# Weights prepared by contraction chunks from a transposed copy, two token blocks projected as the chunks arrive, and the row mean entering by a row of weight sums

## The chip, the cores and the metric

The kernel runs on one core of a Trainium2 chip. The metric is the device time of one execution in microseconds (us); lower is better. All numbers come from timed runs of the kernel before and from one profiled execution of it.

## The reference

What is computed, cut to what matters (x has 2048 rows of 1024, in f32; all matrices are 1024 x 1024):

```python
x = L0_attn_data                                  # (4, 512, 1024)
ln = (x - mean(x)) / sqrt(var(x) + 1e-5)          # over the last axis
block_mask = mask.reshape(32, 32, 32, 32).sum(axis=(1, 3)) > 0   # 32 x 32 squares
w_masked = weight * repeat(repeat(block_mask, 32, 0), 32, 1)
x = x + einsum('bsk,nk->bsn', ln, w_masked)       # the projection
z = (x - mean(x)) / sqrt(var(x) + 1e-5)
logits = z @ W_gate + b_gate                      # 8 experts
top_idx = top_k(logits, 2)
y = relu(einsum('bsd,edh->bseh', z, W_e) + b_e)   # of the two chosen experts
x = x + y.mean over the two
```

## The kernel before, in words

The 2048 rows are 16 token blocks of 128 (`NB`). The kernel has two stages. In the first, each token block is projected, normalised and routed; in the second, 38 blocks of 128 gathered rows go through their experts. Both stages are matrix multiplication in f32r split into a rounded part (HI) and its remainder (LO), in three passes (`PASSES`: HI by HI, HI by LO, LO by HI). A pass over one half (512 columns) of a token block is 8 matmuls, one for each chunk of 128 of the contraction; a block is 2 halves of 3 passes, 48 matmuls.

Every engine has one instruction list, executed in order; semaphores are counted (`wait_ge`, `then_inc`). So an instruction that waits holds up all that stands behind it on its engine.

Before the first projection the weight is prepared, in eight stripes `r` of 128 output rows, each through a chain over all engines. SyncE (SP) loads the mask stripe and the weight stripe, 512 KB each. VectorE (DVE) sums the mask over groups of 32 columns (`sum_mask`, L862); TensorE (PE) sums over groups of 32 rows with a 0/1 matrix (`group_sums`, L353); DVE compares with 0 (`element_mask`, L873); GpSimd (POOL) multiplies the weight stripe with the mask (L1053); ScalarE (ACT) takes the row mean (`mean`, L561) and subtracts it (`centre`, L566), because with centred weight rows the mean of a token drops out of the product; PE transposes the stripe in eight pieces into PSUM (`transpose_w`, L362); ACT copies it, rounded, to `wT` HI (`w_hi`, L571); DVE writes the remainder to `wT` LO (`w_lo`, L868), with one input in PSUM and one in SBUF. PE also multiplies each masked stripe with the gate weights (`fold_w`, L396) so that the logits can be had from x itself. The first half of block 0 is projected after four stripes (`PASS_AT`), the second after all eight. `warm` (L386) is a run of dummy matmuls at the start.

The transposed token blocks come from the host as `data_t`. For each block t, ACT copies them, rounded, to `xT` HI (`x_hi`, L555) and DVE writes the remainder (`x_lo`, L719). ACT computes mean and squares of the row block (`stats1`, L601 and L603), POOL the inverse deviation `kept` (`inverse_std1`, L1020 and L1022). After the projection of a half, DVE adds it, scaled, to the rows (`residual`, L727), and takes the statistics of the sum (`stats2`, L708 and L714), POOL computes `inverse_std2`, ACT writes the normalised rows (L632). The gate product (L475) and the logits (L460) run on PE between the halves; DVE selects two experts (`top2`) and turns positions into one-hot tables (`one_hots`, L775 to L788), PE puts them into the queue (`enqueue`, L380; `positions`, L449).

Each block of the loop is on PE: logits of block i-1, half 0 of block i, `enqueue(i-2)`, the gate product of block i, `positions(i-1)`, half 1 of block i. Half n of block i waits only for `residual(i-1, n)`, which frees the accumulator. ACT has in each turn: `x_hi(i+1)`, the normalised rows, in turns 10 to 14 one or two pieces of the first expert's weight (L637, their remainders on POOL are L1069), `gated` (L641), `stats1(i+1)`.

Of the kernel before, what the change touches and what calls it, by code (L numbers as in the profile page):

```python
# [5 lines left out]
F32 = mybir.dt.float32  # L6
# [15 lines left out]
def build(nc, data, weight, mask, w_gate, b_gate, w_e, b_e, data_t, out):  # L22
# [14 lines left out]
    SNAP = 7  # L37
    N_LATE = N_BLOCKS - EARLY
# [7 lines left out]
    with ctx:  # L46
# [24 lines left out]
        mask_stage = at("mask_stage", [P, NT, D], I32, slot_base + NT * D * 4)  # L71
        w0_stage = at("w0_stage", [P, KT, H], F32, slot_base + slot_bytes // 2)
# [12 lines left out]
        group = sb("group", [P, P], F32)  # L85
        msum_offset = cursor[0]
        msum = sb("msum", [P, NT, NSUB], F32)
        emask = sb("emask", [P, NT, NSUB], F32)
# [14 lines left out]
        fold = sb("fold", [P, 2 * N_EXP], F32)  # L103
# [4 lines left out]
        foldedT = at("foldedT", [P, QUARTER], F32, rows_b_offset)  # L108
        kept = sb("kept", [P, NB], F32)
        minus_mean = sb("minus_mean", [P, NT], F32)  # L110
# [10 lines left out]
        rs = sb("rs", [P, 2, 4], F32)  # L121
# [37 lines left out]
        assert cursor[0] <= msum_offset + 2 * NT * NSUB * 4  # L159
# [61 lines left out]
        l_x, l_raw, l_bias = (even_odd(n) for n in ("l_x", "l_raw", "l_bias"))  # L221
        l_xr, l_x1 = ([sem(f"{n}_{i}") for i in range(3)] for n in ("l_xr", "l_x1"))
# [3 lines left out]
        c_msum, c_em, c_wm, c_wlo = sem("c_msum"), sem("c_em"), sem("c_wm"), sem("c_wlo")  # L226
        c_masked, c_mean = sem("c_masked"), sem("c_mean")
        c_group, c_wt, c_whi = sem("c_group"), sem("c_wt"), sem("c_whi")
# [13 lines left out]
        ST, TOP, HOT, RS1, RS2, GATES = 3, 11, 7, 2, 4, 4  # L242
# [8 lines left out]
        def w_half_of(r):  # L251
            return r % 2

        def x_side(t):
            return psT[:, 0, :, :] if t == NB else xb[:, t % 2, :].rearrange("p (k t) -> p k t", t=P)
# [4 lines left out]
        PASS_AT = NT // 2  # L260
        X0_AT = 4
        WARM = (16, 24, 24)
# [3 lines left out]
        def _(eng):  # L266
            def load_x(t):
                if t >= 2:
                    eng.wait_ge(c_xlo, t - 1)
                    eng.wait_ge(c_gate, t - 1)  # L270
                eng.dma_start(xb[:, t % 2, :], data_t[t]).then_inc(l_x[t % 2], 16)

            for r in range(NT):
                rows = slice(r * P, (r + 1) * P)
                if r == X0_AT:
                    load_x(0)
                eng.dma_start(mask_stage[:, r, :], mask[rows, :]).then_inc(s_m[r], 16)  # L277
                eng.dma_start(w_stage[:, r, :], weight[rows, :]).then_inc(s_w[r], 16)  # L278
# [4 lines left out]
            eng.wait_ge(s_spare, 16)  # L283
# [11 lines left out]
            for i in range(-1, NB + 1):  # L295
                t = i + 1
                if t < NB:
                    if t >= 3:
                        eng.wait_ge(l_x1[t % 3], 16 * (t // 3))
                        eng.wait_ge(c_ln2, t - 2)  # L300
# [829 lines left out]
```

## Time and profile before

| | us |
|---|---|
| median of 3 timed runs | 703.81 |
| lowest and highest | 702.95 and 704.12 |
| the profiled execution's own time | 703.16 |
| its span, from first to last instruction | 701.4 |
| PE busy in the span | 678.8 (97%) |
| DVE, ACT, POOL busy | 297.3, 276.5, 289.2 |
| mean granted TensorE clock | 0.994 |

Time lies outside the span by 1.8 us. A busy time of PE is the time in which some matmul was under way; it tells where PE had no work at all, and not that its work was useful.

### The profile page before, as it was taken

Reading aid. Unit: us, or ns where it says so; the run is one execution under the profiler, and the core shown is the slowest. Engines: PE = TensorE matmul, PEld = TensorE weight load, DVE = VectorE, ACT = ScalarE, POOL = GpSimd, SP = SyncE. Lnnn points to the kernel's source line nnn. Section 1 sums busy time; section 2 is a strip of 40 time slices with the busy share of each in tenths; the row PEclk is TensorE's granted clock in tenths of the full one; section 3 lists DMA queues with packets and bytes.
Section 4 is the critical chain, followed back from the end, with each engine's and each line's share of the span. In section 5 each row is a group of like instructions: output and inputs, shape, how many; then the busy total and the mean of one; then the engine's idle time right before and its main releaser. Section 6 shows DMA issues by size and latency. Waiting matters only on the chain.

```text
span 701.4 us, 11208 instructions
## 1 busy us (share of the span) xinstructions
PE 678.8 (97%) x3617; PEld 558.5 (80%) x3617; DVE 297.3 (42%) x572; ACT 276.5 (39%) x387; POOL 289.2 (41%) x256
## 2 busy tenths in 40 slices
PE   6799999999999999999999999999999999999993
PEld 5568888788888888888888888888888888888882
DVE  4657675777986563342450640360542430000000
ACT  4964343435553334333333333343434343434330
POOL 5512111124763245635363645353545453434330
PEclk9999999999999999999999999999999999999997
DMA  8825445388844388687684774685784854232323
GB/s 314 317 89 189 175 152 209 128 292 270 267 156 151 121 217 252 141 252 163 177 238 125 199 224 82 173 242 135 187 259 97 230 133 110 42 53 38 54 36 54
DMA packets 34501, 118.21 MB, mean 169 GB/s; under 512 B 5776, under 2 KB 5776, under 8 KB 34448
## 3 DMA queue, kind: packets, MB, share of 16 engines
q1 hardware_dynamic: 22032, 80.23, 32.2%
q0 software_dynamic: 11232, 37.23, 26.2%
q8 instruction: 34, 0.56, 0.3%
q10 hardware_dynamic: 1184, 0.04, 0.1%
q14 instruction: 19, 0.16, 0.1%
HBM read 83.40 MB, written 37.75 MB: 173 GB/s over the span
## 4 chain that ended last, share of the span: by engine, by line
PE 94%; DMA 2%; SPq 1%; ACT 0%; DVE 0%; POOLq 0%; issue 0%
PE psO L339 86%; PE psT L442 5%; DMA mask_stage<-L_attn_mask 2%; PE psG L475 1%; SPq L278 1%; SPq L277 1%; PE psT L380 0%; PE psT L460 0%; ACT wT L571 0%; PE psT L362 0%; POOLq L46 0%; PE psS L449 0%; DVE wT L868 0%; DVE msum L862 0%; ACT xb L679 0%
## 5 line engine op out<-in xcount | busy, mean ns | idle before, releaser
L339 PE MATMUL psO<-slots,xT 128*128 (+1 forms) x1872 | 436.2, 392 | 0.0
L339 PEld LDWEIGHTS psO<-slots,xT 128*128 128x128 f32 x1872 | 348.3, 188 | 70.8
L339 PE MATMUL psO<-wT,xT 128*128 128x512 f32 x768 | 182.7, 394 | 0.2 <-ACT wT L571 0.2
L339 PEld LDWEIGHTS psO<-wT,xT 128*128 128x128 f32 x768 | 141.7, 188 | 28.5 <-ACT wT L571 0.3
L1083 POOL DMA_INDIRECT rows_out<-xb,tok_of x37 | 63.1, 1706 | 222.6 <-ACT xb L679 215.2
L679 ACT ACTIVATE xb<-psO 128x512 f32<-128x512 f32 x78 | 46.6, 598 | 253.2 <-PE psO L339 253.2
L850 DVE CAST slots<-raw 128x1024 fp32r<-128x1024 f32 x56 | 56.2, 1003 | 193.5 <-PE psO L339 105.0
L1077 POOL TENSOR_TENSOR xT<-x2T,xT 128x1024 fp32r<-128x1024 f32 x38 | 99.5, 2619 | 18.3 <-ACT x2T L658 18.0
L852 DVE TENSOR_TENSOR slots<-raw,slots 128x1024 fp32r<-128x1024 f32 x56 | 73.1, 1305 | 1.9
L617 ACT ACTIVATE psO<-bias_slot 128x512 f32 (+1 forms) x78 | 47.0, 602 | 37.3 <-ACT xb L679 15.2
L653 ACT ACTIVATE xT<-psT 128x1024 fp32r<-128x1024 f32 x38 | 38.4, 1011 | 7.1 <-PE psT L442 7.1
L658 ACT ACTIVATE x2T<-psT 128x1024 f32<-128x1024 f32 x38 | 38.7, 1017 | 0.0
L1020 POOL TENSOR_SCALAR rs<-squares 128x1 f32<-128x1 f32 x16 | 8.6, 538 | 68.1 <-ACT psT L603 67.9
L555 ACT ACTIVATE xT<-xb 128x1024 fp32r<-128x1024 f32 x16 | 17.0, 1060 | 42.4 <-PE psO L339 40.5
L1032 POOL TENSOR_SCALAR rs<-mv 128x1 f32<-128x1 f32 x16 | 3.8, 236 | 57.9 <-DVE mv L714 46.5
L1045 POOL DMA_INDIRECT x<-x_rows,tok_of x19 | 23.7, 1248 | 6.2 <-DVE tok_of L950 3.1
L1069 POOL TENSOR_TENSOR slots<-w_stage,slots 128x1024 fp32r<-128x1024 f32 x8 | 19.2, 2410 | 9.5 <-ACT slots L637 9.5
L727 DVE SCALAR_TENSOR_TENSOR xr<-psO,kept,xr 128x512 f32<-128x512 f32 x22 | 16.4, 746 | 14.8 <-PE psO L339 14.5
L632 ACT ACTIVATE x<-xr,rs 128x1024 f32<-128x1024 f32 x11 | 13.7, 1242 | 21.9 <-POOL rs L1037 21.9
L719 DVE TENSOR_TENSOR xT<-xb,xT 128x1024 fp32r<-128x1024 f32 x16 | 19.5, 1218 | 1.9 <-ACT xT L555 1.9
L1053 POOL TENSOR_TENSOR w_stage<-w_stage,emask 128x1024 f32<-128x1024 f32 x8 | 15.3, 1912 | 12.1 <-DVE emask L873 12.1
L442 PEld LDWEIGHTS psT<-ident,x 128*128 128x128 f32 x152 | 17.7, 140 | 2.5
(167 smaller groups left out, 448.7 us busy)
## 6 DMA issues: line engine op xcount, KB each, us to landing
raw<-L_ffn_W_e SPq DMA_DIRECT2D x56, 512.0 KB
xb<-data_t SPq DMA_DIRECT2D x16, 512.0 KB, 4.2
x_rows<-x SPq DMA_DIRECT2D x16, 512.0 KB, 5.0
xr<-L_attn_data SPq DMA_DIRECT2D x11, 512.0 KB, 5.7
rows_out<-xr SPq DMA_DIRECT2D x11, 512.0 KB, 2.7
mask_stage<-L_attn_mask SPq DMA_DIRECT2D x8, 512.0 KB, 11.1
w_stage<-L_attn_weight SPq DMA_DIRECT2D x8, 512.0 KB, 11.7
bias_slot<-L_ffn_b_e SPq DMA_DIRECT2D x8, 512.0 KB
```

Source lines behind the costliest of these rows:

```text
L339: last = eng.matmul(psum, xT[:, p, a, kt, :], moving(b, kt), start=(i == 0 and kt == 0 and not seeded), stop=(i == len(PASSES) - 1 and kt ...
L442: last = eng.transpose(psT[:, turn_bank(b), kt, :], rows_of(b, slice(kt * P, (kt + 1) * P)), ident[:])
L617: eng.activation(psO[:, n, :], bias, ACT.Copy).then_inc(c_seed, 1)
L653: eng.activation(xT[:, b % 2, HI, :, :], psT[:, turn_bank(b), :, :], ACT.Copy).then_inc(c_rhi, 1)
L658: eng.activation(x2T[:], psT[:, turn_bank(b), :, :], ACT.Copy).then_inc(c_rhi, 1)
L679: eng.activation(xb[:, b % 2, n * HALF:(n + 1) * HALF], psO[:, n, :], ACT.Relu, scale=1.0 / TOP_K).then_inc(c_out, 1)
L719: eng.tensor_tensor(xT[:, t % 2, LO, :, :], x_side(t), xT[:, t % 2, HI, :, :].bitcast(F32), ALU.subtract).then_inc(c_xlo, 1)
L850: eng.tensor_copy(slots[:, e % 2, HI, kt, :], raw[:, kt % 2, :]).then_inc(c_split, 1)
L852: eng.tensor_tensor(slots[:, e % 2, LO, kt, :], raw[:, kt % 2, :], slots[:, e % 2, HI, kt, :].bitcast(F32), ALU.subtract).then_inc(c_split, 1)
L1045: eng.indirect_dma_start(rows_of(b), None, x2_rows[0:known, :], bass.IndirectOffsetOnAxis(ap=tok_col(b), axis=0), bounds_check=known - 1, ...
L1077: eng.tensor_tensor(xT[:, b % 2, LO, :, :], x2T[:], xT[:, b % 2, HI, :, :].bitcast(F32), ALU.subtract).then_inc(c_rlo, 1)
L1083: eng.indirect_dma_start(out, bass.IndirectOffsetOnAxis(ap=tok_col(b), axis=0), xb[:, b % 2, :], None, bounds_check=N_TOK + P - 1, compute ...
```

## The change

The host passes two more arrays: `weight_t`, the transposed weight, and `mask_blocks`, the mask reordered so that the 1024 elements of one 32 by 32 square lie in one row, and a tile of 128 rows holds the squares of one contraction chunk (128 values of k, all output columns). The weight is prepared by chunk `c` of the contraction, directly in the layout that the product reads:

- A chunk's squares are summed, 1024 to 1, on DVE (`sum_blocks`) or, for chunks 1, 3 and 5, on ACT (`block_sums`); DVE turns the sum into a row of 32 flags with a comparison against a diagonal table (`blocks_of`, a tensor_tensor with both inputs in SBUF); PE spreads it over the 128 partitions (`spread_k`, f16); ACT copies it out (`mask_k`); POOL multiplies the chunk of `weight_t`; ACT rounds it (`w_hi`); DVE takes the remainder (`w_lo`), now with both inputs in SBUF. `mean`, `centre` and the 64 transposes are gone.
- Blocks 0 and 1 are projected together, chunk by chunk (`chunk_hh`, `chunk_lh`, `chunk_hl`), 12 matmuls a chunk, into four PSUM halves (`acc`).
- The weight rows are loaded a second time, untransposed, behind the chunks (`load_w`), masked (`mask_rows`, six on DVE, two on POOL) with row sums, for `fold_w` and for the sums. `row_of_sums` on PE makes a row of weight sums, the same in all partitions.
- The mean of a token block comes in by that row: for blocks 0 to 3 ACT scales it (`move_mean`) and POOL adds it to the finished rows (`correct`); for blocks 4 to 15 ACT writes it, scaled, into the accumulator ahead of the first pass (`seed_mean`), and the passes add to it. Each half then waits for `seed_mean`, which waits for `residual`.
- The order of all engines for blocks 2 to 6 is written out by hand; gates, logits and expert selection of blocks 0 to 3 are done later and together (`top2_first`, `places_first`, `hots_first`). From turn 7 (`LOOP`) the loop is as before, with `seed_mean` added. The expert stage is unchanged.

The core of the diff:

```diff
-        WARM = (16, 24, 24)
+        WARM = (24, 40)
+        SUMS_ACT = (1, 3, 5)
+        ROWS_POOL = (2, 5)
 # SP
+            load_mask(0)
+            load_wt(0)
+            load_x(0)
+            load_mask(1)
+            load_mask(2)
+            load_wt(1)
             load_x(1)
+            for c in range(3, KT):
+                load_mask(c)
+                load_wt(c - 1)
+            load_wt(KT - 1)
+            load_rows(0)
+            load_x(2)
+            load_rows(1)
+            load_w(0)
...
 # PE
+            def chunk(i, c, t):
+                part_x, part_w = PASSES[i]
+                for n in range(NH):
+                    mm = eng.matmul(acc(t, n), xT[:, t, part_x, c, :], wT[:, part_w, c, n * HALF:(n + 1) * HALF],
+                                    start=(i == 0 and c == 0), stop=(i == 1 and c == KT - 1))
...
+            warm(WARM[0])
+            spread_k(0)
+            warm(WARM[1])
+            spread_k(1)
+            chunk_hh(0, 0)
+            chunk_lh(0, 0)
+            chunk_hl(0, 0)
...
+            for c in range(2, KT - 1):
+                if c < 4:
+                    spread_k(c + 2)
+                chunk_hh(c, 0)
+                chunk_hh(c, 1)
+                if c >= 4 and c + 2 < KT:
+                    spread_k(c + 2)
+                if c == KT - 2:
+                    spread_n()
+                chunk_lh(c, 0)
+                chunk_lh(c, 1)
+                chunk_hl(c, 0)
+                chunk_hl(c, 1)
...
+                if i == 0 and t >= FIRST:
+                    eng.wait_ge(c_sown, NH * (t - FIRST) + n + 1)
...
+            project_pass(2, 0, 0)
+            project_pass(2, 0, 1)
+            fold_w(0)
+            fold_w(1)
+            project_pass(2, 0, 2)
+            fold_w(2)
+            project_pass(2, 1, 0)
+            fold_w(3)
+            row_of_sums(0)
+            row_of_sums(1)
...
 # ACT
+            def seed_mean(t, n):
...
+                eng.wait_ge(c_res, NH * (t - 1) + n + 1)
+                eng.activation(psO[:, n, :], sum_row[:, n * HALF:(n + 1) * HALF], ACT.Copy,
+                               scale=minus_mean1[:, t:t + 1]).then_inc(c_sown, 1)
...
+            mask_k(6)
+            w_hi(5)
+            mask_k(7)
+            w_hi(6)
+            mean1(0)
+            w_hi(7)
 # DVE
+            def blocks_of(c):
...
+                eng.tensor_tensor(blocks_k[:, c, :], block_sum[:, c:c + 1].to_broadcast([P, NSUB]), off_diagonal[:],
+                                  ALU.is_gt).then_inc(c_blocks, 1)
+            def w_lo(c):
+                eng.wait_ge(c_whi, c + 1)
+                eng.tensor_tensor(wT[:, LO, c, :], w_stage[:, c, :], wT[:, HI, c, :].bitcast(F32), ALU.subtract).then_inc(c_wlo, 1)
...
+            blocks_of(3)
+            sum_blocks(4)
+            w_lo(2)
+            blocks_of(5)
             w_lo(3)
+            sum_blocks(6)
+            sum_blocks(7)
...
 # POOL
+            for c in range(KT):
+                eng.wait_ge(c_kmask, c + 1)
+                eng.wait_ge(s_w[c], 16)
+                rows = w_stage[:, c, :].rearrange("p (g s) -> p g s", s=SUB)
+                eng.tensor_tensor(rows, rows, k_mask[:, c, :].unsqueeze(2).to_broadcast([P, NSUB, SUB]), ALU.mult).then_inc(c_masked, 1)
+            inverse_std1(0)
+            mask_rows(2)
```

## Rows read from the trace of the kernel before

**Rows 1.** Busy time by stretch: us, then PE, PEld, DVE, ACT, POOL, clock, DMA

```profile
0.00:47.06 47.06, 35.30 (x279) 27.02 (x280) 25.32 (x42) 31.70 (x42) 20.44 (x38) 1.00 0.62 235
47.06:229.33 182.27, 182.27 (x1137) 147.61 (x1137) 134.81 (x382) 79.97 (x114) 58.24 (x100) 1.00 0.58 200
```

**Rows 2.** Chain that ended last: start us, us, what

```profile
9.81 17.06 DMA mask_stage<-L_attn_mask
...
28.58 5.58 PE psO L339 x24
...
41.80 0.22 PE psG L425 x2
...
47.06 5.56 PE psO L339 x24
52.62 0.57 PE psG L475 x16
53.20 0.11 PE psS L449
...
64.61 0.20 PE psT L380 x8
...
95.40 0.13 PE psT L460 x2
...
107.57 0.13 PE psT L460 x2
```

**Rows 3.** Timeline of PE, first 48 us: start, us, engine, line, operation

```profile
7.91 2.75 PE L386 MATMUL psT<-tri,ones 128*128 128x128 f16 x24
...
34.96 0.62 PE L396 MATMUL psS<-w_stage,wg 128*8 128x256 f32 x8
35.51 1.09 PE L362 MATMUL psT<-ident,w_stage 128*128 128x128 f32 x8
```

**Rows 4.** Timeline of DVE, first 62 us

```profile
11.41 1.22 DVE L862 TENSOR_REDUCE msum<-mask_stage 128x32 f32<-128x1024 int32 x1 [0.15 <-DMA mask_stage<-L_attn_mask]
...
26.90 1.22 DVE L862 TENSOR_REDUCE msum<-mask_stage 128x32 f32<-128x1024 int32 x1 [0.65 <-DMA mask_stage<-L_attn_mask]
...
30.40 1.21 DVE L868 TENSOR_TENSOR wT<-psT,wT 128x1024 fp32r<-128x1024 f32 x1
...
56.07 1.22 DVE L785 TENSOR_TENSOR row_hot<-lane,pos_r 128x1024 f16<-128x1024 f16 x1
```

**Rows 5.** Timeline of POOL, first 62 us

```profile
30.56 1.92 POOL L1053 TENSOR_TENSOR w_stage<-w_stage,emask 128x1024 f32<-128x1024 f32 x1 [2.31 <-DVE emask L873]
...
49.38 0.55 POOL L1022 TENSOR_TENSOR kept<-rs,half_neg 128x1 f32<-128x1 f32 x1
...
56.29 1.42 POOL L1022 TENSOR_TENSOR kept<-rs,half_neg 128x1 f32<-128x1 f32 x1
```

**Rows 6.** Timeline of DVE, 168 to 188 us

```profile
175.88 0.16 DVE L777 TENSOR_TENSOR count<-count,psS 128x8 f32<-128x8 f32 x1
175.96 0.72 DVE L778 TENSOR_TENSOR pos_r<-pos_i,low_bits 128x8 int32<-128x8 int32 x1
...
176.79 2.38 DVE L783 TENSOR_TENSOR blk_hot<-lane,pos_j 128x128 f16<-128x128 f16 x1
```

**Rows 7.** Timeline of POOL, 172 to 181 us

```profile
174.24 4.78 POOL L1069 TENSOR_TENSOR slots<-w_stage,slots 128x1024 fp32r<-128x1024 f32 x2 [2.37 <-ACT slots L637]
```

**Rows 8.** Instructions of line L783: count, durations min/median/max in ns, first and last start

```profile
L783 DVE TENSOR_TENSOR blk_hot<-lane,pos_j x16: 291/292/2384, 55.9 to 236.7; 128x128 f16<-128x128 f16 x16
```

**Rows 9.** Timeline of ACT, first 62 us

```profile
28.07 1.05 ACT L561 ACTIVATE rows_a<-w_stage 128x1024 f32<-128x1024 f32 x1
...
38.60 1.02 ACT L571 ACTIVATE wT<-psT 128x1024 fp32r<-128x1024 f32 x1 [0.56 <-PE psT L362]
```

**Rows 10.** Timeline of ACT, 168 to 196 us

```profile
177.39 0.19 ACT L603 ACTIVATION_READ_ACCUMULATOR psT<-xr,minus_mean 128x1 f32 x1
...
180.67 1.06 ACT L555 ACTIVATE xT<-xb 128x1024 fp32r<-128x1024 f32 x1 [3.09 <-PE psO L339]
```

More of the change, by code:

```diff
@@ L19, with build @@
 PASSES = [(HI, HI), (HI, LO), (LO, HI)]
-def build(nc, data, weight, mask, w_gate, b_gate, w_e, b_e, data_t, out):
+def build(nc, data, weight, w_gate, b_gate, w_e, b_e, data_t, weight_t, mask_blocks, out):
     N_TOK, D = data.shape
@@ L37, in build @@
     SNAP = 7
+    FIRST = 4
+    LOOP = 7
     N_LATE = N_BLOCKS - EARLY
@@ L431, in transpose_rows @@
+            positions(4)
+            enqueue(2)
+            project_pass(6, 0, 0)
+            logits(5)
+            project_pass(6, 0, 1)
+            enqueue(3)
+            project_pass(6, 0, 2)
+            gate(6)
+            project_pass(6, 1, 0)
+            enqueue(4)
+            project_pass(6, 1, 1)
+            project_pass(6, 1, 2)
+            positions(5)
             def transpose_rows(b):
@@ new lines, in _ @@
+            block_sums(5)
+            w_hi(3)
+            mask_k(5)
+            w_hi(4)
+            mask_k(6)
[4 more added lines that the diff above has]
+            w_hi(7)
+            square1(0)
+            eng.wait_ge(c_spread_n, 1)
+            eng.activation(n_mask[:].rearrange("p r g -> p (r g)"), psD, ACT.Copy).then_inc(c_nmask, 1)
+            x_hi(2)
+            x_hi(3)
+            stats1(1)
+            for r in range(5):
+                sum_diagonal(r)
@@ L606, in seed_half @@
+            gate_out(4)
+            mean1(5)
+            norm2(3)
+            seed_mean(5, 0)
+            square1(5)
+            x_hi(6)
+            seed_mean(5, 1)
+            norm2(4)
+            gate_out(5)
+            stats1(6)
+            seed_mean(6, 0)
+            x_hi(7)
+            seed_mean(6, 1)
+            norm2(5)
+            stats1(7)
+            gate_out(6)
+            seed_mean(7, 0)
             def seed_half(b, slot, n):
@@ L878, in _ @@
[L878 to L892 removed]
+            FAR = 3.0e38
@@ new lines, in _ @@
+            sum_blocks(6)
+            sum_blocks(7)
+            eng.wait_ge(c_prep, 4)
+            eng.tensor_tensor(blocks_n[:], block_sum[:].unsqueeze(2).to_broadcast([P, KT, P // SUB]),
+                              off_group[:].unsqueeze(1).to_broadcast([P, KT, P // SUB]), ALU.is_gt).then_inc(c_blocks, 1)
+            for c in range(4, KT):
+                w_lo(c)
+            mask_rows(0)
+            mask_rows(1)
+            x_lo(2)
+            residual(0, 0)
+            residual(0, 1)
@@ new lines, in _ @@
+            stats2(3)
+            top2_first()
+            residual(4, 0)
+            stats2_half(4, 0)
+            places_first()
+            hots_first(0)
+            residual(4, 1)
+            stats2_half(4, 1)
+            stats2(4)
+            x_lo(6)
+            hots_first(1)
+            hots_first(2)
+            top2(4)
+            residual(5, 0)
+            stats2_half(5, 0)
+            hots_first(3)
+            residual(5, 1)
+            stats2_half(5, 1)
+            stats2(5)
@@ L907, in _ @@
+            x_lo(7)
+            one_hots(4)
+            top2(5)
+            residual(6, 0)
+            stats2_half(6, 0)
+            one_hots(5)
+            for i in range(LOOP, NB + 1):
+                residual(i - 1, 1)
+                stats2_half(i - 1, 1)
+                stats2(i - 1)
+                top2(i - 1)
                 if i + 1 <= NB:
```

855 lines of the change are left out of this document (590 added, 265 removed).

## The prediction

> **What bounds the kernel now.** I read the busy time by stretch first. From 47.06 us on PE is busy in all of the 182.27 us up to the end of the first stage; before 47.06 it is busy 35.30 us, much of it with dummies, transposes and folding [rows 1]. So time can only be won where PE has no projection to do, and that is the start: by 47.06 us one block is projected, 48 matmuls. The chain shows why: it hangs on the mask's arrival for 17.06 us, and afterwards runs on PE without a break [rows 2]. A pass triple of 24 matmuls takes 5.58 us, 0.2325 each; one block 11.16; a turn of the loop with all its small work takes 107.57 - 95.40 = 12.17. The logits ahead of block 6 end at 107.57 + 0.13 = 107.70, where its first matmul starts [rows 2]. The last mask stripe, the 16th transfer, is used at 26.90 and the third, the 5th transfer, at 11.41 [rows 4]: 1.4 us a transfer.
>
> **The change, part by part.**
>
> *Removed.* 64 transposes, the two ACT instructions a stripe for the mean (1.05 for the mean [rows 9] and about as much for the centring). Their PE time lay in time in which PE waited anyway; what counts is when the projection starts.
>
> *Loading.* The last chunk of `weight_t` is the 18th transfer, two behind the last mask tile, which keeps its place: 26.9 + 2 x 1.3 = 29.5 us. Behind it a mask multiplication (1.92 [rows 5]) and a rounding (1.02 [rows 9]) must come: the last chunk could be multiplied from 32.6, and 12 matmuls of 0.2325 (2.79 us) end at 35.4. That is the floor by the loads. 2.79 a chunk on PE stands against 2 x 1.3 of loading, so PE has no reserve to catch up.
>
> *The start.* Constants, 24 dummies (2.75 us [rows 3], to 7.9), the diagonal table (it waits for an ACT instruction of 1.0), the first sum (1.22, to 9.0), flags, spreading at 9.2; then 40 dummies, 40/24 x 2.75 = 4.6 us, to 13.9; chunk 0 runs from 14.1. Going down the lists with these durations chunk 2 could start at 21.4; six chunks of 2.79 and some 0.7 for the spreads give 38.8 as the end of blocks 0 and 1. Call this end T1.
>
> *A lock between DVE and POOL.* The rows show one. A table of 128x128 takes DVE 0.29 and once 2.38 [rows 8]: that one began at 176.79, and POOL had two multiplications of weight under way from 174.24 to 179.02 [rows 6, 7]. The small instruction ahead, at 175.96, took 0.72 and ended as POOL's first one did. Both have two inputs in SBUF. The instruction at 175.88, with one input in PSUM, took its usual 0.16 [rows 6]. The other way round POOL's power took 1.42 where it takes 0.55, beside a DVE instruction with two SBUF inputs that ended at 57.29 [rows 4, 5]. And `w_lo` with its input in PSUM took 1.21 across a mask multiplication at 30.56, which kept its 1.92 [rows 4, 5]. So the old `w_lo` was free of this and the new one isn't, nor are `x_lo` and `blocks_of`.
>
> The Trainium skill says the same on its page "SBUF — State Buffer", section "Who interferes with whom": a VectorE instruction with two SBUF inputs and a GpSimd instruction that reads SBUF exclude each other for the whole instruction. By that rule the new `w_lo` and `blocks_of` are held up for a whole mask multiplication each time; a sum without it would keep T1 at 38.8.
>
> Per chunk the pair must then do 1.92 + 1.21 + 0.15 = 3.3 us, more than PE's 2.79. Worse, the flags of chunk c+1 stand on DVE behind what waits for POOL's chunk c, and PE's spreading, ACT's copy and the next multiplication hang on them. My walk: multiplications of chunks 2 to 7 at 19.9, 22.5, 25.8, 29.1, 32.5 to 33.9, 37.0 to 38.2; chunk 2 on PE from 24.8. From there PE needs 16.7 + 0.7, to 42.2, and loses some 2 us in chunks 4 and 5: `w_lo(4)` stands on DVE behind the sums of both last mask tiles and behind POOL, and the spreading for chunk 7 stands behind chunk 5's first pass. T1 is 43.8 to 45.6 by who gets the lock in ties. I take 44.
>
> *From T1 on PE.* Up to the first matmul of block 6 it has: blocks 2 to 5, 4 x 11.16 = 44.6; eight foldings of 0.55 (start to start [rows 3]) = 4.4; eight rows of sums, f32 of 128 columns, at half a folding (256 columns) 0.28 = 2.2; the small transposes (0.22 [rows 2]) and two small sums 0.5; six gate products of 0.57 = 3.4 and five logits of 0.13 = 0.7 [rows 2]; three enqueues of 0.20, two positions of 0.11 and a few more for the four blocks [rows 2] = 0.9. Sum 56.7. Before, that matmul stands at 107.70, with one enqueue (0.2) more done. Gain = 107.5 - 56.7 - T1 - S = 50.8 - T1 - S, where S is what PE waits between T1 and block 6. What no row shows: the row of sums could take from 0.13 (logits) to 0.55 (folding) each, 1.2 us less to 2.2 more in all. `mask_rows` with its sum is taken as 1.35 (`w_lo` 1.21 to two halves, 1.5); `correct` on POOL lies between 1.92 [rows 5] and 2.39, half of the 4.78 [rows 7].
>
> *Waits in the hand-written order (S).* Eight `mask_rows`, `correct`, `x_lo` and the expert selection share that lock. `logits(3)` on PE stands behind `gated` of block 3 on ACT, which stands behind `norm2(1)` and `seed_mean(4, 1)`, and these behind POOL's corrections: 0 to 1.2 us. `seed_mean(5, 0)` needs `residual(4, 0)`, behind the selection of four blocks at once on DVE (some 3 us, from POOL's last deviation): 0.3 to 1.2. `positions(4)` and `seed_mean(6, 0)` stand behind `hots_first(2)`, which needs `enqueue(1)`, and `top2(4)`: 1.3 to 2.1. S is 1.6 to 4.5; I take 3. The row weights land by about 46 us at 1.3 each, ahead of their use: cover enough.
>
> *The loop from turn 7.* Same matmuls. `seed_mean` (half of 1.0 plus, about 0.6) comes behind `stats1` on ACT. In a turn with weight pieces ACT ends its statistics at 177.58 and starts `x_hi` at 180.67 [rows 10]; the next half needs the seed just ahead of that: 2.5 us of cover remain. Cost nothing; without the cover, its lateness in every turn. The expert stage moves as a whole.
>
> *Sum.* 50.8 - 44 - 3 = 3.8 us, against the profiled execution's own 703.16 (span 701.4 and 1.8 around it). The median of the runs is 0.65 above it; taken off the median: 700.0 us.
>
> **The rivals.**
>
> *The lock costs little* (0.22): instructions interleave luckily, T1 38.8 and S 2 give a gain of 10: 693.8. For it: POOL's multiplications reach the lock only when flags come, and PE hides some. Against it: the flags themselves are under the lock.
>
> *The loads are the floor* (0.06): T1 35.4, S near 0.5, gain 15: 689. Against it the 40 dummies, and PE's 2.79 a chunk.
>
> *The gain is used up* (0.13): T1 45.6 and S 4.5 give 0.7: 703.1, no change.
>
> *The hand-written order starves PE* (0.08): one wrong place costs more than I found. `mask_rows` 4 to 7 stand among residuals on DVE; if these come 5 us later than PE's foldings want them, S is 8: T1 44 gives a loss of 1.2, 705. It decides from S = 6.8 on.
>
> *`seed_mean` becomes PE's bound in every turn* (0.06), the other side: if ACT's chain slips by more than 2.5 us, each of nine turns waits. At 1 us a turn more than covered that is 9 us, minus the 3.8: 709. It decides from 0.42 us a turn. Against it: ACT is idle 3.1 us just there [rows 10].
>
> The forecast itself has 0.45, its own range 698 to 702.
>
> **How the numbers follow.** A change of under 0.2%, 1.4 us, can't be told from none here. Faster: 0.45 + 0.22 + 0.06 and a little of the used-up case, 0.75. Same: 0.11. Slower: 0.08 + 0.06, 0.14. The range 691 to 704.5 holds the forecast, the used-up case and most of the one without a lock; it leaves out the floor, `seed_mean` as the bound and the outer part of starvation, together under 0.2.
>
> **What would show it.** In the profile after: the end of the 96th chunk matmul (T1) at 44, 38.8 or 35; `w_lo` longer than 1.21 where POOL multiplies, up to 3.1; `blocks_of` up to 2; mask multiplications 3.3 apart in the middle. Block 6's first matmul at 103.9 instead of 107.70. Turns of 12.17 from there on, PE without gaps. Wrong would be: a granted clock that falls in the waits of the start (it is 1.00 in the first 47 us now, with PE idle for 11.8 of them [rows 1]), turns longer than 12.17, or a T1 on time and a gain lost behind it.

## The result, and the profile after

| us | before | after |
|---|---|---|
| median of the runs (9 each) | 703.33 | 705.32 |
| lowest and highest | 702.94, 704.12 | 704.89, 705.80 |
| profiled execution, its span | 703.16, 701.4 | 705.06, 703.3 |

The changed kernel is slower: ratio 1.0027, interval 1.0017 to 1.0038. The forecast was 700.0, faster.

The busy time by stretch of the kernel after (us, then PE, PEld, DVE, ACT, POOL, clock, DMA), beside [rows 1]:

```profile
0.00:47.06 47.06, 36.88 (x188) 28.36 (x189) 34.60 (x43) 22.88 (x36) 26.65 (x38) 0.93 0.91 345
14.00:18.00 4.00, 1.55 (x5) 0.97 (x4) 4.00 (x4) 2.11 (x2) 1.60 (x1) 0.80 1.03 410
18.00:22.00 4.00, 4.00 (x12) 2.80 (x11) 2.79 (x3) 1.23 (x3) 1.92 (x1) 0.50 1.03 410
22.00:26.00 4.00, 3.82 (x16) 2.66 (x15) 1.48 (x3) 2.09 (x4) 1.81 (x1) 0.85 1.03 410
47.06:107.70 60.64, 56.96 (x409) 41.23 (x408) 39.90 (x83) 36.63 (x60) 26.35 (x42) 1.00 0.47 176
107.70:229.33 121.63, 120.64 (x765) 97.10 (x765) 96.52 (x270) 64.66 (x94) 48.14 (x68) 1.00 0.58 203
```

Two things are new. The granted clock is 0.50, 1.2 GHz, between 18 and 22 us, where it was 1.00 before. And behind 47.06 PE is no longer without a gap: 3.7 us are idle up to 107.70, 1.0 behind it.

The timeline of PE of the kernel after shows where:

```profile
16.84 1.22 PE L490 MATMUL psO<-wT,xT 128*128 128x512 f32 x2 [2.45 <-DVE wT L1299]
...
29.06 0.19 PE L476 MATMUL psS<-blocks_k,group 128*128 128x32 f16 x1 [0.63 <-DVE blocks_k L1294]
...
44.40 3.91 PE L457 MATMUL psT<-wT,xT 128*128 128x512 f32 x16
...
91.24 0.19 PE L668 MATMUL psS<-chosen,tri 128*128 128x32 f16 x1 [0.70 <-DVE chosen L1197]
...
93.03 3.89 PE L457 MATMUL psO<-wT,xT 128*128 128x512 f32 x16 [1.43 <-ACT psO L883]
...
107.52 2.09 PE L457 MATMUL psO<-wT,xT 128*128 128x512 f32 x8 [1.35 <-ACT psO L883]
...
226.40 5.74 PE L457 MATMUL psO<-wT,xT 128*128 128x512 f32 x24 [0.80 <-ACT psO L883]
...
231.98 0.29 PE L575 MATMUL psT<-diagonal,gated 128*128 128x16 f32 x2
```

T1, the end of blocks 0 and 1, is 44.40, where the first pass of L457 starts. Block 6's first matmul is the row at 107.52. Before, the chain puts it at 107.70 [rows 2] and PE's timeline at 107.55, so nothing was gained up to there, and the rest loses: the last logits start at 231.98, and at 229.93 before, 2.05 later. The span grew by 1.9.

The lock of the prediction is there. The timeline of DVE of the kernel after (L1294 is `blocks_of`, L1299 `w_lo`, L1557 the mask multiplication):

```profile
13.92 1.73 DVE L1294 TENSOR_TENSOR blocks_k<-block_sum,off_diagonal 128x32 f16<-128x32 f32 x1
15.57 1.21 DVE L1299 TENSOR_TENSOR wT<-w_stage,wT 128x1024 fp32r<-128x1024 f32 x1
...
27.11 1.90 DVE L1294 TENSOR_TENSOR blocks_k<-block_sum,off_diagonal 128x32 f16<-128x32 f32 x1
...
33.34 4.08 DVE L1299 TENSOR_TENSOR wT<-w_stage,wT 128x1024 fp32r<-128x1024 f32 x2
```

And POOL's multiplication of chunk 1:

```profile
13.69 1.92 POOL L1557 TENSOR_TENSOR w_stage<-w_stage,k_mask 128x1024 f32<-128x1024 f32 x1 [2.11 <-ACT k_mask L821]
```

A flag row of 0.18 took 1.73: it began while POOL's multiplication of 13.69 to 15.61 was under way and ended with it. Behind it on DVE stood `w_lo(0)`, for which PE then waited 2.45 us. In that wait the clock fell.

### The profile page after: what moved, and what is told of

Read it like the earlier page. It is cut to its first block, busy times and chain, and to the rows that moved or that the text cites. A ratio compares the mean times of both kernels' runs of the same rounds, so it can differ in the third digit from the quotient of the medians.

```text
span 703.3 us, 11125 instructions
## 1 busy us (share of the span) xinstructions
PE 677.6 (96%) x3571; PEld 552.2 (79%) x3571; DVE 310.5 (44%) x543; ACT 289.1 (41%) x420; POOL 309.5 (44%) x266
## 4 chain that ended last, share of the span: by engine, by line
PE 89%; DVE 5%; issue 2%; ACT 1%; POOL 1%; POOLq 0%; ACTq 0%; DVEq 0%
PE psO L457 78%; PE psT L718 5%; PE psT L457 2%; PE psO L490 1%; PE psT L490 1%; DVE wT L1299 1%; PE psG L563 1%; DVE xT L1089 1%; DVE blocks_k L1294 1%; DVE block_sum L1285 1%; PE psS L545 1%; DVE st L1078 0%; ACT psO L883 0%; PE psT L531 0%; PE psT L554 0%
## 5 line engine op out<-in xcount | busy, mean ns | idle before, releaser
L457 PE MATMUL psO<-slots,xT 128*128 (+1 forms) x1872 | 436.1, 392 | 0.0
L457 PEld LDWEIGHTS psO<-slots,xT 128*128 128x128 f32 x1872 | 348.3, 188 | 70.7
L457 PE MATMUL psO<-wT,xT 128*128 128x512 f32 x624 | 151.5, 396 | 3.6 <-ACT psO L883 3.6
L457 PEld LDWEIGHTS psO<-wT,xT 128*128 128x128 f32 x624 | 114.4, 188 | 27.6 <-issue 4.3
L1598 POOL TENSOR_TENSOR xT<-x2T,xT 128x1024 fp32r<-128x1024 f32 x38 | 98.0, 2580 | 18.3 <-ACT x2T L1025 18.2
L1277 DVE TENSOR_TENSOR slots<-raw,slots 128x1024 fp32r<-128x1024 f32 x56 | 74.9, 1337 | 1.9
L1525 POOL TENSOR_SCALAR rs<-mv 128x1 f32<-128x1 f32 x16 | 5.3, 334 | 54.6 <-DVE mv L1084 54.5
L1557 POOL TENSOR_TENSOR w_stage<-w_stage,k_mask 128x1024 f32<-128x1024 f32 x8 | 18.0, 2249 | 16.1 <-ACT k_mask L821 16.1
L1590 POOL TENSOR_TENSOR slots<-w_stage,slots 128x1024 fp32r<-128x1024 f32 x8 | 19.2, 2413 | 9.5 <-ACT slots L1006 9.5
L811 ACT ACTIVATE xT<-xb 128x1024 fp32r<-128x1024 f32 x12 | 12.7, 1056 | 21.0 <-PE psO L457 17.7
L883 ACT ACTIVATE psO<-raw,minus_mean 128x512 f32<-128x512 f32 x24 | 16.3, 679 | 9.6 <-DVE xr L1097 6.0
L490 PE MATMUL psO<-wT,xT 128*128 128x512 f32 x48 | 16.8, 448 | 3.2 <-DVE wT L1299 3.0
L718 PE MATMUL psT<-ident,x 128*128 128x128 f32 x152 | 19.7, 272 | 0.0
```

The lines of the kernel that those rows point to most:

```text
L457: last = eng.matmul(psum, xT[:, p, a, kt, :], moving(b, kt), start=(i == 0 and kt == 0 and not seeded), stop=(i == len(PASSES) - 1 and kt ...
L490: mm = eng.matmul(acc(t, n), xT[:, t, part_x, c, :], wT[:, part_w, c, n * HALF:(n + 1) * HALF], start=(i == 0 and c == 0), stop=(i == 1 an ...
L718: last = eng.transpose(psT[:, turn_bank(b), kt, :], rows_of(b, slice(kt * P, (kt + 1) * P)), ident[:])
L1277: eng.tensor_tensor(slots[:, e % 2, LO, kt, :], raw[:, kt % 2, :], slots[:, e % 2, HI, kt, :].bitcast(F32), ALU.subtract).then_inc(c_split, 1)
L1598: eng.tensor_tensor(xT[:, b % 2, LO, :, :], x2T[:], xT[:, b % 2, HI, :, :].bitcast(F32), ALU.subtract).then_inc(c_rlo, 1)
```

## The experiments

Every kernel was timed against the kernel before on its own chip, whose median was 703.25 to 703.40. The first five start from the kernel after, each with one edit. "The wait for `w_lo(0)`" is PE's 2.45 us at 14.4 to 16.8.

**Dummies in the wait for `w_lo(0)`**

```diff
             chunk_lh(0, 0)
+            warm(20)
             chunk_hl(0, 0)
```

> Edit: 20 more dummy matmuls (about 2.3 us) on PE between chunk_lh(0, 0) and chunk_hl(0, 0), where PE of the changed kernel stands still for 2.45 us up to 16.84 and its granted clock then reads 0.50 from 18 to 22 us. Theory A (the wait lets the clock fall, and the slow matmuls of chunks 0 and 1, 0.43 us each where 0.23 is usual, delay the spreading for chunk 3): the clock stays 1.00, spread_k(3) comes 2 us earlier than its 23.68, and the end of blocks 0 and 1 (T1, now 44.40) comes 1.5 to 2.5 us earlier; the time falls by 1 to 2.5 us. Rival B (the lock between DVE and POOL alone sets the pace of the chunks, the clock is hidden): the clock is 1.00, T1 moves by under 0.5 us and the time is unchanged. Rival C (what is won at T1 is given back in the hand-written order of blocks 2 to 6): T1 earlier by 2, time within 0.5 us.

Measured: 703.68, ratio 1.000 (0.9991 to 1.001), span 702.0. The clock stayed at 1.00 up to T1, and T1 is 41.38, 3.0 earlier. Only 1.3 of the 3.0 reached the end. The windows of this kernel at 90 us show why:

```profile
90.00:92.00 2.00, 1.99 (x6) 1.64 (x7) 1.97 (x6) 1.98 (x3) 0.73 (x2) 0.64 0.00 0
92.00:94.00 2.00, 2.00 (x6) 1.54 (x6) 1.86 (x4) 0.69 (x1) 0.61 (x2) 0.50 0.31 127
```

And PE's timeline there:

```profile
88.22 0.19 PE L669 MATMUL psS<-chosen,tri 128*128 128x32 f16 x1 [0.71 <-DVE chosen L1198]
...
90.01 5.50 PE L457 MATMUL psO<-wT,xT 128*128 128x512 f32 x16 [1.43 <-ACT psO L884]
```

The same two waits as in the kernel after (0.71, 1.43) were now followed by the lower clock: the 16 matmuls took 5.50, and 3.89 there. So the clock's fall is worth 3.0 us at T1, and the later waits can cost 1.6 more than they last. In the medians of the timed runs the edit is worth 1.6 (705.32 and 703.68).

**Flags with one tensor input in SBUF**, as a tensor_scalar

```diff
-                eng.tensor_tensor(blocks_k[:, c, :], block_sum[:, c:c + 1].to_broadcast([P, NSUB]), off_diagonal[:],
-                                  ALU.is_gt).then_inc(c_blocks, 1)
+                eng.tensor_scalar(blocks_k[:, c, :], off_diagonal[:], block_sum[:, c:c + 1], None, ALU.is_lt).then_inc(c_blocks, 1)
```

> Edit: the flags of a chunk by one tensor_scalar (table below the chunk's sum, the sum as a per-partition scalar), so with one tensor input in SBUF in place of two. Theory A (the lock needs two SBUF inputs on DVE, and the flags behind POOL's multiplications hold up the chain spreading, copy, next multiplication): every instance takes under 0.3 us where four now take 0.66 to 1.90, spread_k(4) and (5) no longer wait (0.63 us at 29.06 now), T1 falls from 44.4 to 41.5 to 43; the time falls by 1 to 2 us if the rest follows. Rival B (DVE waits for POOL whatever its inputs): some instances stay near 2 us and T1 stays. Rival C (T1 earlier, but the order of blocks 2 to 6 gives it back): T1 earlier, time within 0.5 us.

Measured: 705.19, ratio 1.0022 (1.0013 to 1.0031). DVE's rows of this kernel:

```profile
14.00 1.93 DVE L1294 TENSOR_SCALAR blocks_k<-off_diagonal,block_sum 128x32 f16<-128x32 f32 x1
20.26 0.96 DVE L1294 TENSOR_SCALAR blocks_k<-off_diagonal,block_sum 128x32 f16<-128x32 f32 x1 [0.93 <-ACT rows_a L817]
22.38 0.24 DVE L1294 TENSOR_SCALAR blocks_k<-off_diagonal,block_sum 128x32 f16<-128x32 f32 x1
```

The flags were held as before, 1.93, with a table and a scalar for each partition, both in SBUF. This form doesn't escape the lock: the wait for `w_lo(0)` stayed (2.16), and so did the one for a flag row (0.62, at 27.98). T1 is 43.37; the clock fell here too, for a shorter stretch (0.64 from 18 to 22 us, 1.00 from 22 to 26). The Trainium skill, "SBUF — State Buffer", section "Who interferes with whom", names tensor_scalar among the operations that can use VectorE's second port and then contend; the 1.93 agrees, though the trace doesn't show in which way the instruction read its inputs.

**Residuals ahead of the expert selection**

```diff
 # POOL
-            inverse_std2(3)
             inverse_std1(4)
+            inverse_std2(3)
 # DVE
-            top2_first()
             residual(4, 0)
+            top2_first()
             stats2_half(4, 0)
...
-            hots_first(2)
-            top2(4)
             residual(5, 0)
+            hots_first(2)
+            top2(4)
```

> Edit: order alone. DVE adds half 0 of block 4 before the selection of four blocks and half 0 of block 5 before hots_first(2), instead of behind; POOL computes the deviation of block 4 before block 3's second one. Theory A (PE's 1.43 us before block 5 and 1.35 before block 6 are seed_mean standing behind a residual that stands behind selection work): both gaps vanish (the first leaves the 0.7 us for the selection's matmuls), and as PE never waits again before turn 7 the time falls by 2.3 to 2.8 us, to just below the kernel before. Rival B (other waits take their place: positions, enqueue, later blocks): the gaps vanish but reappear within the next two blocks, and the time falls by under 1 us.

Measured: 701.00, ratio 0.9964 (0.9952 to 0.9975), span 699.6. The waits of 1.43 and 1.35 are gone, 0.69 for `chosen` stays. The PE timeline of this kernel has the first pass of block 5 directly behind the small matmuls:

```profile
90.58 0.19 PE L668 MATMUL psS<-chosen,tri 128*128 128x32 f16 x1 [0.69 <-DVE chosen L1197]
...
90.79 3.90 PE L457 MATMUL psO<-wT,xT 128*128 128x512 f32 x16
```

The span is 3.7 shorter: T1 is 43.74, 0.7 earlier, which this edit doesn't explain (the start ran a little differently), and from T1 to block 6 it is 60.0 instead of 63.1, 2.8 of it the two waits. So the order of a few instructions of DVE and POOL, each under a microsecond, was worth 3.0 us.

**The seed of the last half ahead of `x_hi(16)`**

```diff
                 if i + 1 <= NB:
                     x_hi(i + 1)
-                if i < NB:
+                if i < NB - 1:
                     seed_mean(i, 1)
```

with `if i == NB - 1: seed_mean(i, 1)` ahead of these lines.

> Edit: order alone. In the last turn ACT writes the seed of block 15's half 1 before x_hi(16), which waits for the transposed rows of the expert stage. Theory A (PE's 0.80 us at 226.40 is this seed standing behind x_hi(16)): the gap vanishes and the time falls by 0.8 to 1.0 us. Rival B (x_hi(16) coming 0.7 us later delays the first expert's passes by as much): the gap vanishes and comes back before the expert stage, time unchanged.

Measured: 704.12, ratio 1.001 (1.0001 to 1.0019), span 701.1. The last turn takes 13.01 (logits at 216.71 and 229.72), as before, where the kernel after has 14.00. In this profile the clock behaved the other way round from the kernel after. The same wait at the start was not followed by the lower clock, T1 is 41.60, but the waits at 90 were:

```profile
16.68 0.73 PE L490 MATMUL psO<-wT,xT 128*128 128x512 f32 x2 [2.45 <-DVE wT L1301]
...
90.20 5.50 PE L457 MATMUL psO<-wT,xT 128*128 128x512 f32 x16 [1.42 <-ACT psO L883]
```

Of the program's order nothing differs up to 90 us. So the fall of the clock is not fixed by the program: these waits expose the kernel to it, execution by execution. The 11 timed runs say the same: four took 702.8 to 703.0 at a mean clock of 0.993, seven took 704.0 to 704.6 at 0.990 to 0.991. With the dummies none of 11 was below 0.992; the nine of the kernel after were all at 0.988 to 0.990. This also confirms T1: without the fall it is 41.4 to 41.6, with and without dummies.

**Jobs exchanged**: DVE multiplies by the mask, read straight from the PSUM tile that PE spread it into, and POOL takes the remainder `w_lo`; `mask_k` on ACT goes, `spread_k` now waits for DVE's multiplications, and `spread_n` comes one place later.

```diff
 # DVE
+            def mask_chunk(c):
+                eng.wait_ge(c_spread, c + 1)
+                eng.wait_ge(s_w[c], 16)
+                rows = w_stage[:, c, :].rearrange("p (g s) -> p g s", s=SUB)
+                eng.tensor_tensor(rows, rows, psB(c).unsqueeze(2).to_broadcast([P, NSUB, SUB]), ALU.mult).then_inc(c_masked, 1)
 # POOL
             for c in range(KT):
+                eng.wait_ge(c_whi, c + 1)
+                eng.tensor_tensor(wT[:, LO, c, :], w_stage[:, c, :], wT[:, HI, c, :].bitcast(F32), ALU.subtract).then_inc(c_wlo, 1)
```

> Edit: the two engines under the lock change jobs. DVE multiplies the chunk of weight with the spread mask read straight from PSUM (one SBUF input, ACT's copies of the mask go), POOL takes the remainder (two SBUF inputs, 2.4 us where it converts). So beside POOL's remainders DVE has, but for x_lo(0), x_lo(1) and the small flags, no instruction with two SBUF inputs. Theory A (the lock sets the pace of the chunks): chunk 2 starts at 20 to 22 instead of 25.1, POOL's remainders follow each other without being stretched, T1 is 36 to 38.5. Rival B (the loads and the hops between five engines set the pace): T1 stays above 41. What follows T1 is unchanged: if the hand-written order passes all of it on, the time falls by 6 us or more; if its own waits on DVE, ACT and POOL decide (rival C), by 2 to 3.

Measured: 704.55, ratio 1.0012 (1.0003 to 1.002), span 701.5, T1 42.64. POOL's eight remainders are no longer stretched, they take 2.37 to 2.40 each, but PE has seven waits of 0.28 to 1.25 in the chunks (4.0 us in all), and T1 is 1.3 later than with the dummies. The lock is not gone. DVE's flags still have both inputs in SBUF, and four of the rows took 1.21 to 1.87 beside POOL's remainders; one from each timeline:

```profile
12.98 1.87 DVE L1286 TENSOR_TENSOR blocks_k<-block_sum,off_diagonal 128x32 f16<-128x32 f32 x1
```

```profile
12.43 2.37 POOL L1555 TENSOR_TENSOR wT<-w_stage,wT 128x1024 fp32r<-128x1024 f32 x1 [7.31 <-ACT wT L825]
```

So this run doesn't tell the lock's price from that of the chain PE, DVE, ACT, POOL and back.

**Dummies, residuals and last seed together**, the three edits as above.

> Edit: the 20 dummies, the early residuals and the last turn's seed together, nothing else. By the single runs: T1 41.4; the waits before blocks 5 and 6 (1.43 and 1.35) and in the last turn (0.80) gone; and if what slowed the matmuls after those waits in two of the profiles (granted clock 0.50 from 92 to 94 us, 1.6 us lost) was the clock falling in them, no stretch below 1.00 after 30 us. The terms add: span 703.3 - 3.0 - 2.8 - 0.3 - 0.95 = 696.3, time 698. If they overlap (a rival: each uncovers the next wait), 700 or more.

Measured: 698.33 (697.86 to 698.66), ratio 0.9926 (0.9913 to 0.9938), span 696.4. The parts add up: 3.0 for the clock, 3.0 for the residuals, 0.96 for the last seed are 7.0, and 703.3 - 7.0 = 696.3. The clock is 1.00 throughout. PE's timeline of this kernel tells what sets T1:

```profile
16.44 0.73 PE L490 MATMUL psO<-wT,xT 128*128 128x512 f32 x2 [1.25 <-DVE wT L1302]
...
23.05 0.19 PE L476 MATMUL psG<-blocks_k,group 128*128 128x32 f16 x1 [1.31 <-DVE blocks_k L1297]
...
31.57 0.73 PE L490 MATMUL psO<-wT,xT 128*128 128x512 f32 x2 [0.53 <-DVE wT L1302]
...
41.38 0.93 PE L457 MATMUL psT<-wT,xT 128*128 128x512 f32 x3
```

From chunk 2 (23.15) to T1 lie 18.2 us: 72 matmuls at 0.2325 are 16.7, one wait 0.5, and the spreads and changes of operand between them 1.0. So from chunk 2 on PE sets the pace, and the lock costs at most 0.5 there. What else it costs lies ahead of chunk 2: the wait for `w_lo(0)`, of which the dummies leave 1.25, and the 1.31 for a flag row that took 1.35. How much of these waits is the lock's, no run isolates.

**The exchange with these orders**

> Edit: the exchange of jobs between DVE and POOL with the early residuals and the last turn's seed, no dummies added. If T1 of the exchange (36 to 38.5) is passed on: span 692 to 694. If blocks 2 to 6 then wait for row weights, folds and corrections on the other engines, new waits stand on PE between T1 and block 4, and the span is 695 or more.

The edits are those of the two kernels ahead, without dummies. Measured: 699.24, ratio 0.9939 (0.9926 to 0.9952), span 697.4, T1 42.66: 0.9 slower than the one with the jobs as they were. The T1 of 36 to 38.5 on which the expectation rests didn't come. The clock was at 1.00 here (0.60 from 14 to 18 us in the profile of the exchange alone), and T1 is the same: in these two profiles it doesn't hang on the clock.

**Foldings in one run**: the eight `fold_w` and eight `row_of_sums` of the kernel after stand two at a time between passes; here they all follow `project_pass(3, 0, 0)`.

```diff
+            for n in range(2):
+                for i in range(3):
+                    project_pass(2, n, i)
+            project_pass(3, 0, 0)
+            for r in range(NT):
+                fold_w(r)
+            for r in range(NT):
+                row_of_sums(r)
```

> Edit: order of PE alone. The eight foldings and eight rows of sums, spread between the passes of blocks 2 and 3 in the changed kernel, come in one run behind the first pass of block 3. Question: in the changed kernel a pass of 8 matmuls between such small f32 groups takes 2.0 to 2.05 us from start to start of its neighbours, where 8 x 0.2325 is 1.86. Theory A (each change between the two kinds costs some 0.15 us): the passes of block 2 take 1.86, and from T1 to the first logits PE needs 0.8 to 1.0 us less. Rival B (the small groups themselves have been misjudged, the passes are not longer): no difference. The time falls by at most 1 us.

Measured: 702.31 (700.22 to 705.22), ratio 0.9985 (0.9972 to 0.9998), span 698.6, with T1 41.36. PE of this kernel:

```profile
41.36 11.16 PE L457 MATMUL psT<-wT,xT 128*128 128x512 f32 x48
52.36 1.97 PE L457 MATMUL psO<-wT,xT 128*128 128x512 f32 x8
54.27 3.64 PE L545 MATMUL psS<-row_stage,wg 128*8 128x256 f32 x64
57.84 2.05 PE L554 MATMUL psT<-bias_slot,ones 128*128 128x128 f32 x16
59.65 2.08 PE L457 MATMUL psO<-wT,xT 128*128 128x512 f32 x8
```

Eight foldings take 57.84 - 54.27 = 3.57, 0.45 each, and 48 matmuls of the projection 11.00. From T1 to the first logits (73.28 in the kernel after) it is 27.18 against 28.88, so the same matmuls cost 1.7 us less when they aren't mixed, more than theory A had. The span is 4.7 shorter: 3.0 at T1, where the clock stayed at 1.00 in this profile, and these 1.7. The spread of the timed runs, 5 us, fits a clock that falls in none, one or both of the places where PE waits: mean clock 0.995 in the runs of 700.2 to 700.8, 0.990 to 0.993 around 702.3, 0.987 from 704.0 on.

**The flags' table in PSUM**, on top of the three orders: `blocks_of` has one input in SBUF and one in PSUM.

```diff
+        psX = psT[:, 1, KT // 2, 0:NSUB]
-                eng.tensor_tensor(blocks_k[:, c, :], block_sum[:, c:c + 1].to_broadcast([P, NSUB]), off_diagonal[:],
+                eng.tensor_tensor(blocks_k[:, c, :], block_sum[:, c:c + 1].to_broadcast([P, NSUB]), psX,
```

> Edit: the kernel with dummies, early residuals and the last turn's seed (698.33), and the diagonal table that the flags are compared with moved from SBUF to PSUM, so that blocks_of has one input in SBUF and one in PSUM. The tensor_scalar form with its one tensor input in SBUF was still held up to 1.93 us, so the form with fewer SBUF inputs is not the whole rule. Theory A (any DVE instruction with a PSUM input goes free beside POOL, and the held-up flags pace the chunks): every blocks_of takes under 0.25 us, T1 falls from 41.38 to 39.5 to 40.5, the time to 696.5 to 697.5. Rival B (w_lo and x_lo take the lock anyway, POOL's multiplications are then held instead): flags under 0.25 us, T1 within 0.4 of 41.38, time within 0.5 of 698.33.

Measured: 700.29, ratio 0.9951 (0.9938 to 0.9964), span 699.2: worse than with the three orders alone (698.33). The flags are free, 0.17 to 0.19 each, and chunk 2 starts at 22.32. But what was held is now the next DVE instruction with both inputs in SBUF. L1303 is `w_lo` here, L1335 `blocks_n`, the flags for the row weights, whose table stayed in SBUF. DVE first:

```profile
14.02 2.92 DVE L1303 TENSOR_TENSOR wT<-w_stage,wT 128x1024 fp32r<-128x1024 f32 x1
...
24.44 2.81 DVE L1303 TENSOR_TENSOR wT<-w_stage,wT 128x1024 fp32r<-128x1024 f32 x1
...
29.87 1.84 DVE L1335 TENSOR_TENSOR blocks_n<-block_sum,off_group 128x32 f16<-128x32 f32 x1
31.64 2.35 DVE L1303 TENSOR_TENSOR wT<-w_stage,wT 128x1024 fp32r<-128x1024 f32 x2
```

PE, where it waits for `w_lo(4)`, the first of the two at 31.64:

```profile
32.91 0.73 PE L491 MATMUL psO<-wT,xT 128*128 128x512 f32 x2 [2.44 <-DVE wT L1303]
```

POOL's multiplications, with three in a row:

```profile
21.40 7.63 POOL L1561 TENSOR_TENSOR w_stage<-w_stage,k_mask 128x1024 f32<-128x1024 f32 x3 [0.41 <-ACT k_mask L823]
29.76 1.91 POOL L1561 TENSOR_TENSOR w_stage<-w_stage,k_mask 128x1024 f32<-128x1024 f32 x1 [0.73 <-ACT k_mask L823]
```

And the window behind PE's wait:

```profile
34.00:38.00 4.00, 4.00 (x13) 2.86 (x12) 0.95 (x1) 2.12 (x4) 1.85 (x1) 0.57 1.03 410
```

`w_lo(0)` takes 2.92 behind a free flag, where it took 1.21 behind a held one, and PE's pass on it starts at 16.99, no earlier than with the three orders (16.44). `w_lo(3)` takes 2.81, but it isn't what PE waits for at 32.91. That is `w_lo(4)`, and ahead of it stands `blocks_n`, 1.84 beside POOL's multiplication of 29.76 where it took 0.19 with the three orders. PE's pass starts 1.34 later than there (32.91 and 31.57), and in the four microseconds from 34 on the granted clock was 0.57: from that pass to T1 it is 11.36 instead of 9.81. Together that makes T1 44.27 instead of 41.38. Theory B had the flags free and nothing won, but not this loss.

**Exchange, orders and foldings**, with eight dummies, and two sums moved:

```diff
             blocks_of(5)
-            sum_blocks(6)
             mask_chunk(4)
-            sum_blocks(7)
+            sum_blocks(6)
             mask_chunk(5)
+            sum_blocks(7)
```

> Edit: the exchange of jobs again (DVE masks from PSUM, POOL takes remainders), now with the masks of chunks 4 and 5 on DVE ahead of the sums of mask tiles 6 and 7 instead of behind them (in the first try chunk 4 waited at 30.37 for a mask queued behind the tile 6 sum), 8 dummies in chunk 0, early residuals, last turn's seed and the folds in one run. Theory A (with the lock out of the way the loads pace): T1 38 to 39.5 and the time 3 us below the kernel with the same orders and the old jobs. Rival B (the hops PE to DVE to ACT to PE to POOL and PE's own order of spreads pace it): T1 40.5 or more, time no better than that kernel's.

Measured: 697.18, ratio 0.9907 (0.9893 to 0.9922), span 695.5, T1 42.34. That is rival B's T1. The time is 1.2 below the kernel with the three orders, but this one has the foldings in one run as well; against the same with the old jobs, which comes next, it gains nothing.

**Orders and foldings, jobs as in the kernel after**: the edits of dummies, residuals, last seed and foldings.

> Edit: the kernel with dummies, early residuals and the last turn's seed (698.33), and the folds and rows of sums in one run. By the single run from T1 to the first logits it saves 28.90 - 27.18 = 1.7 us. If that carries through: 696.6. If the earlier logits then wait for ACT or the selection on DVE (rival): a part of it, 697.5 or more.

Measured: 696.85 (696.46 to 696.91), ratio 0.9904 (0.9889 to 0.9918), span 694.7, T1 41.46. This is the fastest one. Its first window, with the clock at 1.00:

```profile
0.00:47.06 47.06, 37.51 (x221) 29.64 (x222) 37.11 (x47) 25.87 (x43) 28.45 (x40) 1.00 0.95 372
```

The runs of the two kernels last told don't overlap, but their intervals do; that the unexchanged one is better by 0.3 us rests on 4 runs each.

**The same with the table in PSUM and later positions**

```diff
+            project_pass(5, 0, 0)
             eng.wait_ge(c_top4, 12)
...
-            project_pass(5, 0, 0)
             project_pass(5, 0, 1)
-            enqueue(0)
             project_pass(5, 0, 2)
+            enqueue(0)
```

> Edit: the one before it, plus the flag table in PSUM, plus the position matmuls of the first four blocks behind the first pass of block 5 instead of ahead of it (0.7 us of waiting for the selection), with enqueue(0) one pass later. If all terms add: 696.6 less 1 for the flags less 0.6, 695.0. If the selection chain (hots, enqueues, top2 of block 4) now comes late for positions(4), a wait before block 6 returns and the last term is lost: 695.7.

Measured: 699.07, ratio 0.9932 (0.992 to 0.9944), span 697.4. The table in PSUM brings back the wait of 2.44 (at 32.49), with `blocks_n` taking 1.85, the lower clock behind it (0.69 from 34 to 38 us) and T1 43.83. `w_lo(3)` took 2.09 here and the wait is the same, so it doesn't come from the 2.81. The later positions end the wait of 0.70 ahead of them and leave one of 0.74 ahead of block 6.

## Why the prediction was wrong

**The lock, and T1.** Right in direction, and the number hit: 44 forecast, 44.40 measured; `blocks_of` up to 1.90 (forecast 2), a pair of `w_lo` 4.08. The Trainium skill's page "SBUF — State Buffer", section "Who interferes with whom", on which the forecast drew, agrees with these rows where both DVE inputs lie in SBUF. But the walk reached the number in part by luck. Without the clock's fall T1 is 41.4, 2.6 less than the walk: chunk 2 starts at 23.15 instead of 24.8, and from there it is 18.2 instead of 19.2, because the 2 us that the walk lost in chunks 4 and 5 are 0.5. With the fall it is 44.4. "A granted clock that falls in the waits of the start" stood in the forecast only under "Wrong would be", with no price and no chance. The argument against it was that the clock of the kernel before stayed at 1.00 with PE idle for 11.8 us there [rows 1]. That row didn't bear on it: it adds up many waits. The longest behind PE's first matmul is this one, in the timeline of PE of the kernel before, and the kernel after has one of 2.45:

```profile
23.21 0.41 PE L353 MATMUL psG<-msum,group 128*128 128x32 f32 x2 [1.57 <-DVE msum L862]
```

**From T1 to block 6: the first step that failed.** "S is 1.6 to 4.5; I take 3", and "Sum 56.7". Measured: 107.52 - 44.40 = 63.1, of which PE was idle 3.7 (0.70, 1.43, 1.35, and 0.2 in small ones) and busy 59.4. The waits are those that the forecast named: `seed_mean` behind `residual`, behind the selection on DVE. The two longer ones were worth 3.0 us. So S was 0.7 more than the 3 taken, within its range, and the term that was mis-sized is the work: 2.7 more than the 56.7 summed. The forecast took each matmul of a pass at 0.2325 and the f32 groups at the nearest rows. The groups cost no more than that: eight foldings and eight rows of sums took some 6.0 from start to start, where it had 6.6. The passes did: the 24 of blocks 2 to 5 took some 46.8 from start to start, where it had 44.6. A pass of eight between small groups takes 1.93 to 2.05, where eight times 0.2325 is 1.86. Of the excess, 1.7 came back when foldings and rows of sums stood in one run. That the rest, passes of 1.94 to 2.04 between gates, logits and enqueues, has the same cause was not tested.

**Behind block 6: the second step that failed.** "The loop from turn 7 ... Cost nothing", and turns of 12.17 from block 6's first matmul on. The loop costs nothing in turns 8 to 14: from 132.91 to 217.98 the kernel after has seven turns of 12.153, against 12.17 before. Around them the kernel loses 2.2. In turn 6, which is still written out by hand and for which the sum has no term, from block 6's first matmul to the next logits, 12.84 against 12.03: one enqueue more (0.2), the logits of block 5, now in between (0.14), and 0.5 for passes cut into eights. In turn 7, 12.55 against 12.16: half of it is a wait of 0.20 for `chosen`. In the last turn, 14.00 against 13.02: `seed_mean(15, 1)` stands on ACT behind `x_hi(16)`, which waits for transposed rows that PE makes only between the halves. The timeline of ACT of the kernel after:

```profile
224.74 1.02 ACT L811 ACTIVATE xT<-psT 128x1024 fp32r<-128x1024 f32 x1 [8.59 <-PE psT L718]
225.66 0.69 ACT L883 ACTIVATE psO<-raw,minus_mean 128x512 f32<-128x512 f32 x1
```

The forecast looked for the seed's cover in the turn in the middle and never at the one where the source of `x_hi` changes.

**The sum with measured terms.** 107.5 - 44.4 - 63.1 is 0.0 gained up to block 6, where the forecast had 3.8: 0.4 went at T1, 0.7 in the waits, 2.7 in the work. Behind it 2.0 is lost.

**The rivals.** "The gain is used up" is what happened up to block 6, for its own reason (T1 45.6 and S 4.5) only in part: T1 44.4, S 3.7 and 2.7 of mis-sized work. "The hand-written order starves PE" had the other side right, but its mechanism, `mask_rows` late for the foldings, didn't occur: there is no such wait. "The lock costs little" has more to it than its verdict: with the clock kept up T1 is 41.4, in the middle between 38.8 and 44. `seed_mean` as the bound in every turn is refuted by the 12.153.

**What stays open.** Why the clock falls after a given wait in one execution and not in another; those of the kernel after were seen with and without it. And how much T1 could still give ahead of chunk 2: three ways round the lock (no second SBUF tensor, a PSUM operand, jobs exchanged) gave nothing or less, but each left DVE instructions with both inputs in SBUF to run beside POOL (`w_lo`, `blocks_of` or `blocks_n`). No kernel was run without the lock, so its price stays open.

## What to carry to other kernels

When an order is written out by hand, price each small instruction by who stands behind it: two moves of a few lines and twenty dummies turned 1.0027 into 0.9926, more than any way round the contention between two engines. A wait of TensorE that a change brings into a busy stretch can have a second price, the lower clock behind it, and belongs in the sum with a chance of its own; filling one with dummies brought T1 forward by 3.0 us here, and the median by 1.6. And check an "added at no cost" instruction in the first and the last turn of a loop, where what stands ahead of it has another source.

## What the runs showed of the hardware that wasn't expected

- The granted clock went to half, 1.2 GHz, after a single wait of PE of 2.2 to 2.5 us in an otherwise busy stretch, or after 0.71 and 1.43 with small matmuls between (or 0.34 and 1.25, where jobs were exchanged), and in other executions it did not (1.00 after the same 2.45). Where it fell, the next 16 matmuls took 5.50 instead of 3.89.
- A DVE instruction with one tensor and a per-partition scalar, both in SBUF, was held by POOL (1.93, and 0.24 when free) as one with two tensors was. One with an operand in PSUM was not (0.17 to 0.19).
- Taking an instruction out of this contention passes the hold on to the next one with both inputs in SBUF: with the flags free, `w_lo` took 2.92 and 2.81 instead of 1.21, and another flag table 1.84 instead of 0.19.
- f32 matmuls of 128 and 256 columns set between the passes cost more than their own time: 1.7 us for sixteen groups, gone when they stand together.
